# Attention on one core: all 96 query and key rows loaded into every sixth partition, by SyncE, with no row copies on chip

## The chip, the cores and the metric

The kernel runs on one core of a Trainium2 chip. The metric is the device time of one execution, in microseconds (us). Engines are named as the profile names them: PE (TensorE, PEld is its weight load), DVE (VectorE), ACT (ScalarE), POOL (GpSimd) and SP (SyncE, which here only issues DMAs). "ACTq" and "SPq" are the DMA-issuing instructions of ACT and SP.

## The reference, cut to what matters

The input is x [16 batches, 512 places, 256 channels]. A layer norm with a modulation per batch gives h; attention with 16 heads of width 16 follows, then a norm with a gate, then a mixture of 8 experts of which 2 are taken. The attention part, whose scores are what this change touches, is

```
q, k, v = heads(h @ Wq + bq), heads(h @ Wk + bk), heads(h @ Wv + bv)
scores = einsum('bhqd,bhkd->bhqk', q, k)
rel_q = einsum('bhld,lrd->bhlr', q, pos_emb)      # pos_emb[l, r] = dist_emb[l - r + 255], clipped
rel_k = einsum('bhrd,lrd->bhlr', k, pos_emb)
probs = softmax((scores + rel_q + rel_k) / 4)
ctx = einsum('bhqk,bhkd->bhqd', probs, v)
```

Everything is float32. To multiply float32 numbers at bfloat16 speed with small error, q and k are each split into three bfloat16 parts, and a score is a sum over six pairs of parts: 6 pairs x 16 channels = 96 rows of one matmul.

## The kernel before

The program is a row of stages: modulation, projections (which also store the parts of q and k to memory), distances (which stores rel_q + rel_k as a matrix of 512x512 for each of the 256 heads, "the matrix", in r_scratch), attention, and experts. The change touches only the attention stage, which works through 256 heads (16 batches of 16), one after another.

**A head.** For each of four query tiles t, PE multiplies the 96 rows of the tile's queries (t_qa) with the 96 rows of the keys (t_kb) into one of two PSUM buffers (t_ps): `score`, L1060. DVE adds the matrix (t_r), negates, and takes the row minimum (t_low): `add`, L1153, a custom operation and a read of its accumulator, with a small MEMSET (L1152) ahead. `score` of tile k waits until `add` of tile k-2 has emptied the buffer. POOL subtracts the minimum for tiles 0 and 1 (L952), ACT for tiles 2 and 3 (L1205). PE transposes the result one head later (`turn`, L1072, four transposes a tile), ACT takes the exponential (L1215), and PE multiplies with the values (`weigh`, L1083). Per group of four heads there are also the row sums (PE L1094), their reciprocal (DVE L1163), its widening (POOL L966), a transpose (PE L1101), the scaling (DVE L1168) and the store (SPq L1024). So a group of four heads is 16 scores, 16 turns, two blocks of `weigh` of 16 recorded matmuls each, and one each of the rest; 64 groups make the stage.

**The rows.** t_qa and t_kb have 96 partitions and hold two batches. Six blocks of 16 partitions hold the parts of q in the order 0, 1, 2, 0, 1, 0 and those of k in the order 0, 0, 0, 1, 1, 2. Memory holds each part once, 48 rows for q and 48 for k. ACT loads 64 of the 96 rows of each (T_Q_LOADED and T_K_LOADED: one run of 32 rows and two of 16; each row is 8 KB for half a batch, eight heads), 12 DMAs a batch, one after each of the first twelve heads of the batch before. The other 32 rows are copied on chip: those of q by DVE (`copy_q`, L1176, two heads' worth in a copy, one copy in every other head, after tile 1), those of k by POOL (`copy_k`, L986, four heads' worth in a copy, four copies a batch). PE waits for both kinds (q_copied, k_copied) before a new group of four heads.

**The matrix.** SP loads 1 MiB a head in four DMAs of 256 KB (`load_r`, L1008) into a ring of six heads; the load of head n waits until `add` of head n-6 is done. The values (L1014) and the stores (L1024) go through the same SP queue.

**The start of the stage.** ACT issues the 12 loads of batch 0 while SP issues the first heads' matrix; DVE copies three times and POOL twice before the first score, and POOL twice more after it.

Of the kernel before, what the change touches and what calls it, by code (L numbers as in the profile page):

```python
# [20 lines left out]
F32 = mybir.dt.float32  # L21
# [7 lines left out]
H = 16  # L29
D = E // H  # L30
M = 256
KC = E // P
TT = S // P
# [49 lines left out]


A_RUNS, B_RUNS = rows_of(A_PARTS), rows_of(B_PARTS)

T_PAIR = 2 * D
T_Q_LOADED, T_Q_COPY = ((0, 0, T_PAIR), (4 * D, 2 * D, D), (5 * D, 0, D)), T_PAIR
T_K_LOADED, T_K_COPY = ((0, 0, T_PAIR), (2 * D, 2 * D, D), (3 * D, 0, D)), 2 * T_PAIR


def modulation(nc, ins, mod_d, tab_d):
# [763 lines left out]
def attention(nc, rows_d, v_d, r_d, cT_d, nb=NB):  # L856
# [6 lines left out]
    with ctx:  # L863
# [9 lines left out]
        GH = 4  # L873
# [26 lines left out]

        ident_zero = sem("t_ident_zero")
        ident_done = sem("t_ident_done")
        batch_loaded = [sem(f"t_batch_loaded{i}") for i in range(2)]
        BATCH = 16 * (len(T_Q_LOADED) + len(T_K_LOADED))
        K_PLACES, Q_FIRST = (10, 12, 15, 18), 10
        q_copied = sem("t_q_copied")
        k_copied = sem("t_k_copied")
        v_loaded = [sem(f"t_v_loaded{i}") for i in range(2)]
        v_copied = sem("t_v_copied")
        r_loaded = [sem(f"t_r_loaded{i}") for i in range(RR)]  # L910
# [13 lines left out]
        scaled = sem("t_scaled")  # L924
        ctx_stored = [sem(f"t_ctx_stored{i}") for i in range(CS)]
        STORE = 16 * GH

        def rounds(engine, step_of, heads_after):

# [10 lines left out]
        with nc.Block() as block:  # L940
            @block.gpsimd
            def _(pool):
                nc.gpsimd.memset(vx[:], 1.0).then_inc(ident_zero, 1)
                nc.gpsimd.memset(ident[:], 0.0).then_inc(ident_zero, 1)
                pool.wait_ge(ident_zero, 2)
                nc.gpsimd.affine_select(out=ident[:], in_=ident[:], compare_op=ALU.not_equal, fill=1.0,
                                        base=0, pattern=[[-1, P]], channel_multiplier=1).then_inc(ident_done, 1)

                def subtract(n, j, t):

                    pool.wait_ge(added, TT * n + t + 1)
                    nc.gpsimd.tensor_scalar(neg[:, j % RING, t, :], neg[:, j % RING, t, :],  # L952
                                            low[:, j % RING, t:t + 1], None, ALU.subtract).then_inc(pool_sub, 1)

                def copy_v(step, k):
                    G = 2 * step + k

                    pool.wait_ge(v_loaded[k], 16 * (step + 1))
                    later(pool, weighed, TT * (G - 1))
                    nc.gpsimd.tensor_copy(vx[:, k, :, :, 0, :], vv[:, k]).then_inc(v_copied, 1)  # L960

                def widen(G):

                    pool.wait_ge(inverted, G + 1)
                    later(pool, spread, G)
                    nc.gpsimd.tensor_copy(wide[:], inv[:].rearrange("p t j -> p (t j)").unsqueeze(2)  # L966
                                          .to_broadcast([P, GT, CT])).then_inc(widened, 1)

                def head(step, j):
                    n = U * step + j  # L970
                    fixed = isinstance(n, int)
                    if not fixed or n < NH:
                        for t in range(2):
                            subtract(n, j, t)
                    if j % GH == 1 and (not fixed or 2 * GH <= n):
                        widen(2 * step + j // GH - 2)
                    if j % GH == 1 and (not fixed or n < NH):
                        copy_v(step, j // GH)

                def copy_k(b, i, subtracted):  # L980
                    heads = slice(b % 2 * H + GH * i, b % 2 * H + GH * (i + 1))

                    if i % 2 == 0:
                        pool.wait_ge(batch_loaded[i // 2], BATCH * (b + 1))
                    later(pool, pool_sub, subtracted)
                    nc.gpsimd.tensor_copy(  # L986
                        kb[T_K_COPY:T_K_COPY + T_PAIR, :, heads, :].rearrange("r c h w -> r c (h w)").bitcast(F32),
                        kb[0:T_PAIR, :, heads, :].rearrange("r c h w -> r c (h w)").bitcast(F32)).then_inc(k_copied, 1)
                    pool.wait_ge(k_copied, BG * b + i + 1)

                pool.wait_ge(ident_done, 1)
                for i in range(BG):
                    copy_k(0, i, 0)
                for n in range(NH + GH + 2):
                    head(n // U, n % U)
                    for i, place in enumerate(K_PLACES):
                        b = (n - place) // H + 1
                        if (n - place) % H == 0 and 1 <= b < nb:
                            copy_k(b, i, 2 * (n + 1))

            @block.sync
            def _(sp):
# [24 lines left out]
                def batch(g, pair, u):  # L1027
                    b = 2 * pair + u
                    for j in range(H):
                        load_r(g, H * b + j, j)  # L1030
                        k = j // GH
                        if j % GH == 0:
                            load_v(b, k)
                        if j % GH == 1 and BG * b + k >= 4:
                            store(b + (k - 4) // BG, (k - 4) % BG)

# [16 lines left out]
            def _(pe):  # L1053
# [68 lines left out]
                        if k % GT == 9 and (not fixed or 0 <= G < NGR):  # L1122
                            widen(G)

                pe.wait_ge(q_copied, 2)
                pe.wait_ge(k_copied, 1)
                score(0, 0, 0)

                def batch(b, last=False):
                    for s in range(H // U):  # L1130
                        for j in range(U):
                            if j % GH == GH - 1 and not (last and s == H // U - 1 and j == U - 1):
                                pe.wait_ge(q_copied, 2 * (BG * b + (U * s + j) // GH + 2))
                                pe.wait_ge(k_copied, BG * b + (U * s + j) // GH + 2)
                            head(H // U * b + s, j)

                batch(0)
# [7 lines left out]
            def _(dve):  # L1145
# [21 lines left out]
                    dve.wait_ge(spread, G + 1)  # L1167
                    nc.vector.tensor_tensor(cs[:, G % CS, :], cs[:, G % CS, :], p_i[:], ALU.mult).then_inc(scaled, 1)  # L1168

                def copy_q(b, m):  # L1170
                    at = b % 2 * H + 2 * m
                    heads = slice(at, at + 2)

                    if m % 4 == 0:
                        dve.wait_ge(batch_loaded[m // 4], BATCH * (b + 1))
                    nc.vector.tensor_copy(  # L1176
                        qa[T_Q_COPY:T_Q_COPY + T_PAIR, 0, heads, :].rearrange("r h w -> r (h w)").bitcast(F32),
                        qa[0:T_PAIR, 0, heads, :].rearrange("r h w -> r (h w)").bitcast(F32)).then_inc(q_copied, 1)

                def head(step, j):  # L1180
                    n = U * step + j
                    fixed = isinstance(n, int)
                    for t in range(TT):
                        k = TT * j + t
                        if not fixed or n < NH:
                            add(n, j, t, step)
                        b, m = (n - Q_FIRST) // H + 1, (n - Q_FIRST) % H // 2
                        if t == 1 and n % 2 == 0 and b < nb:
                            copy_q(b, m)
                        G = 2 * step + k // GT - 2  # L1190
                        if k % GT == 5 and (not fixed or 0 <= G < NGR):
                            invert(G)
                        if k % GT == 11 and (not fixed or 0 <= G < NGR):
                            scale(G)

                for m in range((H - Q_FIRST) // 2):
                    copy_q(0, m)
                rounds(dve, head, GH + 3)

            @block.scalar  # L1200
            def _(act):
# [31 lines left out]
                    if j % GH == GH - 1 and (not fixed or 7 <= n):  # L1233
                        empty(2 * step + j // GH - 1)

                pieces = [(qa, rows_d[0], run) for run in T_Q_LOADED] + [(kb, rows_d[1], run) for run in T_K_LOADED]

                def load(b, half, piece):
                    u = b % 2
                    tensor, src, (row, stored, rows) = pieces[piece]  # L1240
                    first = H // 2 * half
                    act.dma_start(
                        tensor[row:row + rows, 0, u * H + first:u * H + first + H // 2, :].rearrange("r h w -> r (h w)"),
                        src[b, stored:stored + rows, first:first + H // 2].rearrange("r h w -> r (h w)")
                    ).then_inc(batch_loaded[half], 16)

                def batch(b, last=False):
                    for s in range(H // U):
                        for j in range(U):
                            head(H // U * b + s, j)  # L1250
                            at = U * s + j
                            if at < 2 * len(pieces) and not last:
                                if at == 0:

                                    later(act, scored, TT * H * b)
                                load(b + 1, at // len(pieces), at % len(pieces))

                for half in range(2):
                    for piece in range(len(pieces)):
                        load(0, half, piece)  # L1260
                batch(0)
                for b in range(1, nb - 1):
                    batch(b)
                batch(nb - 1, last=True)
                for j in range(GH):
                    head(NH // U, j)

# [572 lines left out]
```

## Time and profile before

| | us |
|---|---|
| median of 3 runs (2884.1 to 2892.21) | 2888.73 |
| the profiled execution's own time | 2886.97 |
| its span | 2885.2 |

| busy over the span | PE | DVE | ACT | POOL |
|---|---|---|---|---|
| us | 2521.4 | 2055.5 | 1627.6 | 1883.5 |
| share | 87% | 71% | 56% | 65% |

The attention stage lies between 1185.8 us (its first DMA) and about 2250 us. The shares over the span are means over stages with different limits, so only rows from inside the stage speak on this change. In the rows "idle before" is the idle time of the engine ahead of an instruction, with what ended it; a matmul's end is modelled, its start is recorded. Rows of the timeline merge neighbours of one kind (x4).

### The profile page before, as it was taken

What the parts mean: (1) busy time and instruction counts of PE and PEld (TensorE: products, weight loads), DVE (VectorE), ACT (ScalarE), POOL (GpSimd) and SP (SyncE); (2) the same over time, 40 slices, a digit from 0 to 9 for tenths busy, and PEclk for the clock granted to TensorE, in tenths of its full rate; (3) what the DMA queues carried; (4) which work ended last, traced back from release to release, by engine and by line L of the source; (5) the groups of instructions that cost most, each with busy time, mean ns of one, the idle gap of its engine ahead of it and who ended that gap; (6) DMA issues with size and microseconds to landing.
All of it is one profiled execution on the core that took longest, in us unless ns stands there. A gap on an engine that the chain in (4) does not pass through costs nothing. (4 is left out here: it accounts for less than half of the span.)

```text
span 2885.2 us, 53492 instructions
## 1 busy us (share of the span) xinstructions
PE 2521.4 (87%) x19084; PEld 1753.8 (61%) x19084; DVE 2055.5 (71%) x5771; ACT 1627.6 (56%) x2069; POOL 1883.5 (65%) x1535
## 2 busy tenths in 40 slices
PE   3988688788878888599999999999999499999998
PEld 1655477677767777366666666666666355555553
DVE  4767277667767777577777777777777388888885
ACT  1645556566556666277878778788877222222222
POOL 2333356565765564488888888888888356666664
PEclk7999777778778778599999999999999799999999
DMA  3688799999999999999999999999998312222210
GB/s 117 226 296 269 259 401 386 378 400 385 398 393 387 376 404 388 316 328 317 302 313 308 312 310 306 304 306 301 314 301 266 132 68 77 77 77 77 77 48 24
DMA packets 301960, 773.59 MB, mean 268 GB/s; under 512 B 37608, under 2 KB 104496, under 8 KB 258048
## 3 DMA queue, kind: packets, MB, share of 16 engines
q1 hardware_dynamic: 277152, 660.82, 66.6%
q10 hardware_dynamic: 17888, 86.27, 9.2%
q0 software_dynamic: 6656, 23.07, 2.3%
q8 instruction: 154, 2.52, 0.4%
q14 instruction: 110, 0.90, 0.1%
HBM read 417.39 MB, written 352.63 MB: 267 GB/s over the span
## 5 line engine op out<-in xcount | busy, mean ns | idle before, releaser
L952 POOL TENSOR_SCALAR t_neg<-t_neg,t_low 128x512 f32<-128x512 f32 x512 | 793.6, 1563 | 121.5 <-DVE t_low L1153 117.2
L1153 DVE CUSTOM_DVE_ANT_1 t_neg<-t_ps,t_r 128x512 f32<-128x512 f32 x1024 | 667.6, 686 | 250.5 <-issue 245.5
L1215 ACT ACTIVATE t_eT<-t_pt 128x1024 f32<-128x1024 f32 x512 | 524.3, 1024 | 211.6 <-PE t_pt L1072 211.0
L1072 PE MATMUL t_pt<-t_ident,t_neg 128*128 128x128 f32 x4096 | 617.3, 273 | 4.7 <-POOL t_neg L952 4.2
L1072 PEld LDWEIGHTS t_pt<-t_ident,t_neg 128*128 128x128 f32 x4096 | 516.4, 142 | 82.9 <-POOL t_neg L952 5.9
L1537 PE MATMUL e_pX<-e_we,e_h2T 128*128 128x512 f32 x1024 | 455.8, 596 | 14.3 <-DVE e_even L1745 14.3
L1060 PE MATMUL t_ps<-t_kb,t_qa 96*128 96x512 bf16 x1024 | 399.1, 390 | 62.0 <-DVE t_low L1153 37.2
L831 DVE TENSOR_TENSOR d_r<-d_pq,d_r 128x1024 f32<-128x1024 f32 x256 | 299.6, 1219 | 139.0 <-ACT d_r L804 103.8
L1205 ACT ACTIVATE t_neg<-t_neg,t_low 128x512 f32<-128x512 f32 x512 | 369.2, 721 | 46.3 <-DVE t_low L1153 46.3
L831 DVE TENSOR_TENSOR ad_nat<-d_pq,ad_nat 128x1024 f32<-128x1024 f32 x256 | 298.6, 1218 | 121.0 <-ACT ad_nat L804 99.5
L706 POOL COPY ad_nat<-ad_nat 32x2048 f32<-32x2048 f32 (+1 forms) x156 | 294.3, 1886 | 104.6 <-DMA ad_nat<-q_by_place_scratch 98.3
L804 ACT ACTIVATE ad_nat<-d_pk 128x1024 f32<-128x1024 f32 x256 | 251.7, 1024 | 182.4 <-PE d_pk L755 78.5
L804 ACT ACTIVATE d_r<-d_pk 128x1024 f32<-128x1024 f32 x256 | 251.1, 1025 | 152.4 <-DMA r_scratch<-d_r 80.1
L1537 PEld LDWEIGHTS e_pX<-e_we,e_h2T 128*128 128x128 f32 x1024 | 188.6, 190 | 234.8 <-issue 203.7
L743 PE MATMUL d_pq<-ad_tab,ad_nat 96*128 96x128 bf16 x3072 | 292.8, 251 | 19.8 <-DVE ad_nat L831 5.7
L743 PEld LDWEIGHTS d_pq<-ad_tab,ad_nat 96*128 96x128 bf16 x3072 | 229.4, 114 | 58.6 <-issue 24.8
L755 PE MATMUL d_pk<-ad_tab,d_k 96*128 96x128 bf16 x2048 | 178.7, 238 | 83.3 <-ACT ad_nat L804 47.3
L1083 PE MATMUL t_pc<-t_eT,t_vx 128*32 128x512 f32 x2048 | 246.2, 598 | 0.3 <-ACT t_eT L1215 0.3
L706 POOL COPY d_q<-d_q 32x2048 f32<-32x2048 f32 (+1 forms) x52 | 98.1, 1887 | 221.2 <-DMA d_q<-q_by_place_scratch 219.5
L1060 PEld LDWEIGHTS t_ps<-t_kb,t_qa 96*128 96x128 bf16 x1024 | 115.5, 113 | 207.4 <-issue 129.8
L755 PE MATMUL d_pk<-ad_tab,ad_k 96*128 96x128 bf16 x2048 | 202.0, 256 | 25.2 <-ACT ad_nat L804 11.9
L755 PEld LDWEIGHTS d_pk<-ad_tab,d_k 96*128 96x128 bf16 x2048 | 136.1, 106 | 110.0 <-ACT ad_nat L804 61.2
(156 smaller groups left out, 3269.6 us busy)
## 6 DMA issues: line engine op xcount, KB each, us to landing
t_r<-r_scratch SPq DMA_DIRECT2D x1024, 256.0 KB, 6.5
r_scratch<-d_r SPq DMA_DIRECT2D x128, 1024.0 KB, 9.3
r_scratch<-ad_nat SPq DMA_DIRECT2D x128, 1024.0 KB, 7.0
ad_nat<-q_by_place_scratch ACTq DMA_DIRECT2D x78, 256.0 KB, 6.3
q_rows_scratch<-a_part SPq DMA_DIRECT2D x16, 768.0 KB, 4.7
k_rows_scratch<-a_part SPq DMA_DIRECT2D x16, 768.0 KB, 6.7
q_by_place_scratch<-ad_nat SPq DMA_DIRECT2D x6, 2048.0 KB, 16.8
k_by_place_scratch<-ad_nat SPq DMA_DIRECT2D x6, 2048.0 KB, 19.4
```

What stands on the lines that cost most here:

```text
L706: nc.gpsimd.tensor_copy(x[row:row + rows].rearrange("r l n -> r (l n)").bitcast(F32), x[source:source + rows].rearrange("r l n -> r (l n)" ...
L743: last = nc.tensor.matmul(pq[n % 2][:, a, :], q[c][:, l % QW, :], rhs, start=True, stop=True)
L755: last = nc.tensor.matmul(pk[n % 2][:, a, :], k[u][:, c % QW, :], tab[:, at:at + TB], start=True, stop=True)
L804: nc.scalar.activation(r[i % 2][:, :, n * KR:(n + 1) * KR], pk[n % 2][:].rearrange("p r l -> p l r"), ACT.Copy).then_inc(k_out, 1)
L831: nc.vector.tensor_tensor(part, pq[n % 2][:], part, ALU.add).then_inc(q_added, 1)
L952: nc.gpsimd.tensor_scalar(neg[:, j % RING, t, :], neg[:, j % RING, t, :], low[:, j % RING, t:t + 1], None, ALU.subtract).then_inc(pool_sub, 1)
L1060: nc.tensor.matmul(p_s[t % 2][:], lhs, kb[:, :, n % SLOTS, :], start=True, stop=True).then_inc(scored, 1)
L1072: last = nc.tensor.transpose(p_t[t // 2][:, t % 2, c, :], neg[:, j % RING, t, c * P:(c + 1) * P], ident[:])
L1153: nc.vector.tensor_tensor_reduce(out=neg[:, j % RING, t, :].rearrange("p (c r) -> p c r", r=TB), in0=p_s[t % 2][:].rearrange("p (c r) -> p ...
L1205: nc.scalar.activation(neg[:, j % RING, t, :], neg[:, j % RING, t, :], ACT.Identity, bias=low[:, j % RING, t:t + 1], scale=-1.0).then_inc( ...
L1215: nc.scalar.activation(to, p_t[half][:], ACT.Exp, scale=(1.0 if half else -1.0)).then_inc(exped, 1)
L1537: last = nc.tensor.matmul(pX[n][:], h2T[:, u, k, t * P:(t + 1) * P], we[:, k, n * 2 * E:(n + 1) * 2 * E], start=(k == 0), stop=(k == KC - 1))
```

## The change

All 96 rows of q and of k are loaded, and nothing is copied on chip. The rows are laid out otherwise: pair i of the six pairs of parts goes to the partitions i, i+6, i+12, ... (`tensor[pair:ROWS:NPAIR]`), so each DMA writes 16 partitions that stand six apart; the sum over 96 rows is the same. A batch takes 24 DMAs of 16 rows (128 KB each), 3 MiB instead of 2 MiB. For batches after the first, SP issues them, two after the matrix loads of each of twelve heads, in the queue that the matrix uses. ACT issues those of batch 0 only. PE waits for a half batch's twelve DMAs once in eight heads. `copy_q`, `copy_k` and their semaphores are gone.

```diff
-T_Q_LOADED, T_Q_COPY = ((0, 0, T_PAIR), (4 * D, 2 * D, D), (5 * D, 0, D)), T_PAIR
-T_K_LOADED, T_K_COPY = ((0, 0, T_PAIR), (2 * D, 2 * D, D), (3 * D, 0, D)), 2 * T_PAIR
...
-        batch_loaded = [sem(f"t_batch_loaded{i}") for i in range(2)]
-        BATCH = 16 * (len(T_Q_LOADED) + len(T_K_LOADED))
-        K_PLACES, Q_FIRST = (10, 12, 15, 18), 10
+        batch_loaded = [[sem(f"t_batch_loaded{u}_{half}") for half in range(2)] for u in range(2)]
+        NPAIR = len(A_PARTS)
+        HALF = 16 * 2 * NPAIR
+        AHEAD = 6
...
+        def load_rows(engine, b, half, pair, x):
+
+            tensor, parts = ((qa, A_PARTS), (kb, B_PARTS))[x]
+            first = H // 2 * half
+            at = b % 2 * H + first
+            engine.dma_start(tensor[pair:ROWS:NPAIR, 0, at:at + H // 2, :].rearrange("d h w -> d (h w)"),
+                             rows_d[x][b, parts[pair] * D:(parts[pair] + 1) * D, first:first + H // 2
+                                       ].rearrange("d h w -> d (h w)")).then_inc(batch_loaded[b % 2][half], 16)
...
-                    for i, place in enumerate(K_PLACES):
-                        b = (n - place) // H + 1
-                        if (n - place) % H == 0 and 1 <= b < nb:
-                            copy_k(b, i, 2 * (n + 1))
...
+                        done, step = divmod(H * b + j - AHEAD, H)
+                        if 0 <= done < nb - 1 and step < 2 * NPAIR:
+                            if step == 0:
+
+                                later(sp, scored, TT * H * done)
+                            for x in range(2):
+                                load_rows(sp, done + 1, step // NPAIR, step % NPAIR, x)
...
-                pe.wait_ge(q_copied, 2)
-                pe.wait_ge(k_copied, 1)
+                pe.wait_ge(batch_loaded[0][0], HALF)
...
-                            if j % GH == GH - 1 and not (last and s == H // U - 1 and j == U - 1):
-                                pe.wait_ge(q_copied, 2 * (BG * b + (U * s + j) // GH + 2))
-                                pe.wait_ge(k_copied, BG * b + (U * s + j) // GH + 2)
+                            if j == U - 1 and not (last and s == H // U - 1):
+
+                                pe.wait_ge(batch_loaded[(b + s) % 2][1 - s], HALF * ((b + s) // 2 + 1))
...
-                        if t == 1 and n % 2 == 0 and b < nb:
-                            copy_q(b, m)
...
                 for half in range(2):
-                    for piece in range(len(pieces)):
-                        load(0, half, piece)
+                    for pair in range(NPAIR):
+                        for x in range(2):
+                            load_rows(act, 0, half, pair, x)
```

DVE, inside the attention stage before, around the copy after tile 1 of an even head (L1153 is `add`, L1152 its small MEMSET):

```order
L1153 ISA t_neg,t_low<-t_ps,t_r 128x512
L1153 ISA t_low 128x1
L1176 COPY t_qa<-t_qa 32x512
L1152 MEMSET t_tiny 128x1
L1153 ISA t_neg,t_low<-t_ps,t_r 128x512
L1153 ISA t_low 128x1
```

DVE, the same place of the changed kernel (`add` is L1146 there):

```order
L1146 ISA t_neg,t_low<-t_ps,t_r 128x512
L1146 ISA t_low 128x1
L1145 MEMSET t_tiny 128x1
L1146 ISA t_neg,t_low<-t_ps,t_r 128x512
L1146 ISA t_low 128x1
```

The copy between two adds is gone, and the adds stand next to each other; nothing else moves on DVE.

SP before, two groups of heads inside the stage (t_r is the matrix, t_v the values, ctx_scratch the stored context):

```order
L1008 DMA t_r<-r_scratch 128x512 x4
L1024 DMA ctx_scratch<-t_cs 16x512 x4
L1008 DMA t_r<-r_scratch 128x512 x12
L1014 DMA t_v<-v_scratch 128x256
L1008 DMA t_r<-r_scratch 128x512 x4
L1024 DMA ctx_scratch<-t_cs 16x512 x4
```

SP of the changed kernel, two heads with row loads and the store behind them (L995 is the matrix's load, L928 a row load, L1011 the store):

```order
L995 DMA t_r<-r_scratch 128x512 x4
L1001 DMA t_v<-v_scratch 128x256
L928 DMA t_qa<-q_rows_scratch 16x4096
L928 DMA t_kb<-k_rows_scratch 16x4096
L995 DMA t_r<-r_scratch 128x512 x4
L928 DMA t_qa<-q_rows_scratch 16x4096
L928 DMA t_kb<-k_rows_scratch 16x4096
L1011 DMA ctx_scratch<-t_cs 16x512 x4
```

Behind each head's four matrix loads now stand two row loads, in twelve heads of sixteen; the loads that ACT issued between its activations are gone.

POOL before, one piece of the stage (L952 is the subtraction, L966 widens, L960 copies the values):

```order
L960 COPY t_vx<-t_v 128x16x16
L952 TENSOR_SCALAR t_neg<-t_neg,t_low 128x512 x2
L986 COPY t_kb<-t_kb 32x1024
L952 TENSOR_SCALAR t_neg<-t_neg,t_low 128x512 x4
L986 COPY t_kb<-t_kb 32x1024
L952 TENSOR_SCALAR t_neg<-t_neg,t_low 128x512 x2
```

POOL of the changed kernel:

```order
L970 COPY t_wide<-t_inv 128x512
L964 COPY t_vx<-t_v 128x16x16
L956 TENSOR_SCALAR t_neg<-t_neg,t_low 128x512 x8
L970 COPY t_wide<-t_inv 128x512
L964 COPY t_vx<-t_v 128x16x16
```

The eight subtractions of a group of four heads now follow one another with no key copy between them.

## Rows read from the trace of the kernel before

**Rows 1.** Busy time by stretch, granted clock, DMA share, GB/s (distances; attention).
```profile
700.00:1260.00 560.00, 448.68 (x5042) 382.19 (x5044) 395.06 (x481) 324.29 (x342) 341.68 (x194) 0.76 0.99 377
1300.00:2200.00 900.00, 870.22 (x6630) 594.28 (x6629) 667.68 (x2869) 719.28 (x938) 791.03 (x608) 1.00 1.03 308
```

**Rows 2.** Waits from 1300 to 2200 us: who waited, us, times, longest.
```profile
DVE t_neg L1153 <- issue: 214.5, 111, 1.9
...
PE t_ps L1060 <- DVE t_low L1153: 29.8, 110, 0.5
```

**Rows 3.** Copies (ns min/median/max) and the subtraction's group (busy, mean).
```profile
L1176 DVE COPY t_qa<-t_qa x128: 416/418/1252, 1199.5 to 2217.0; 32x512 f32<-32x512 f32 x128
...
L986 POOL COPY t_kb<-t_kb x64: 1029/1032/1210, 1199.6 to 2195.1; 32x1024 f32<-32x1024 f32 x64
...
L952 POOL TENSOR_SCALAR t_neg<-t_neg,t_low 128x512 f32<-128x512 f32 x512 | 793.6, 1563 | 121.5 <-DVE t_low L1153 117.2
```

**Rows 4.** Timeline of PE, one group of four heads: start, us, instruction.
```profile
1504.12 1.92 PE L1083 MATMUL t_pc<-t_eT,t_vx 128*32 128x512 f32 x16
...
1509.73 0.38 PE L1060 MATMUL t_ps<-t_kb,t_qa 96*128 96x512 bf16 x1
...
1510.86 0.41 PE L1060 MATMUL t_ps<-t_kb,t_qa 96*128 96x512 bf16 x1 [0.31 <-DVE t_low L1153]
...
1515.49 0.38 PE L1060 MATMUL t_ps<-t_kb,t_qa 96*128 96x512 bf16 x1
...
1516.15 0.38 PE L1060 MATMUL t_ps<-t_kb,t_qa 96*128 96x512 bf16 x1
...
1517.19 0.41 PE L1060 MATMUL t_ps<-t_kb,t_qa 96*128 96x512 bf16 x1 [0.22 <-DVE t_low L1153]
...
1519.19 0.60 PE L1072 MATMUL t_pt<-t_ident,t_neg 128*128 128x128 f32 x4
...
1520.38 0.64 PE L1083 MATMUL t_pc<-t_eT,t_vx 128*32 128x512 f32 x4
```

**Rows 5.** Timeline of DVE in the same group, around copies and scaling.
```profile
1507.81 0.42 DVE L1176 COPY t_qa<-t_qa 32x512 f32<-32x512 f32 x1
1508.27 0.69 DVE L1153 CUSTOM_DVE_ANT_1 t_neg<-t_ps,t_r 128x512 f32<-128x512 f32 x1
...
1509.50 0.69 DVE L1168 TENSOR_TENSOR t_cs<-t_cs,t_pi 128x512 f32<-128x512 f32 x1
...
1515.99 0.42 DVE L1176 COPY t_qa<-t_qa 32x512 f32<-32x512 f32 x1
1516.44 0.69 DVE L1153 CUSTOM_DVE_ANT_1 t_neg<-t_ps,t_r 128x512 f32<-128x512 f32 x1
```

**Rows 6.** Timeline of POOL in the same group.
```profile
1515.39 3.11 POOL L952 TENSOR_SCALAR t_neg<-t_neg,t_low 128x512 f32<-128x512 f32 x2 [0.70 <-DVE t_low L1153]
1518.56 1.03 POOL L986 COPY t_kb<-t_kb 32x1024 f32<-32x1024 f32 x1
```

**Rows 7.** DMA queues: SP's waits (1300:2200); t_r's issue ns min/median/max; its landing.
```profile
SPq L1008 <- DVE t_low L1153: 264.8, 190, 3.5
...
L1008 SPq DMA_DIRECT2D t_r<-r_scratch x1024: 319/432/3526, 1185.8 to 2223.2; - x171
...
DMA to landing us min/median/max: 2.5/6.5/19.5
```

**Rows 8.** Start of the stage: two stretches, then the timeline.
```profile
1190.00:1206.00 16.00, 3.44 (x6) 0.60 (x6) 5.81 (x16) 1.21 (x2) 2.33 (x2) 0.50 1.03 186
1206.00:1214.00 8.00, 3.79 (x17) 2.71 (x17) 2.66 (x12) 2.46 (x4) 7.44 (x6) 0.53 1.06 387
...
1201.14 1.02 PE L1060 MATMUL t_ps<-t_kb,t_qa 96*128 96x512 bf16 x2 [24.82 <-DVE t_qa L1176]
...
1208.38 0.06 DVE L1152 MEMSET t_tiny<- 128x1 f32 x1 [3.00 <-DMA t_r<-r_scratch]
...
1208.63 4.66 POOL L952 TENSOR_SCALAR t_neg<-t_neg,t_low 128x512 f32<-128x512 f32 x3
```

More of the change, by code:

```diff
@@ L85 @@
 A_RUNS, B_RUNS = rows_of(A_PARTS), rows_of(B_PARTS)
-T_PAIR = 2 * D
-T_Q_LOADED, T_Q_COPY = ((0, 0, T_PAIR), (4 * D, 2 * D, D), (5 * D, 0, D)), T_PAIR
-T_K_LOADED, T_K_COPY = ((0, 0, T_PAIR), (2 * D, 2 * D, D), (3 * D, 0, D)), 2 * T_PAIR
 def modulation(nc, ins, mod_d, tab_d):
@@ L902, in attention @@
         ident_done = sem("t_ident_done")
-        batch_loaded = [sem(f"t_batch_loaded{i}") for i in range(2)]
-        BATCH = 16 * (len(T_Q_LOADED) + len(T_K_LOADED))
-        K_PLACES, Q_FIRST = (10, 12, 15, 18), 10
-        q_copied = sem("t_q_copied")
-        k_copied = sem("t_k_copied")
+        batch_loaded = [[sem(f"t_batch_loaded{u}_{half}") for half in range(2)] for u in range(2)]
+        NPAIR = len(A_PARTS)
+        HALF = 16 * 2 * NPAIR
+        AHEAD = 6
         v_loaded = [sem(f"t_v_loaded{i}") for i in range(2)]
@@ L978, in head @@
                         copy_v(step, j // GH)
[L980 to L989, printed above, removed]
                 pool.wait_ge(ident_done, 1)
-                for i in range(BG):
-                    copy_k(0, i, 0)
                 for n in range(NH + GH + 2):
                     head(n // U, n % U)
-                    for i, place in enumerate(K_PLACES):
-                        b = (n - place) // H + 1
-                        if (n - place) % H == 0 and 1 <= b < nb:
-                            copy_k(b, i, 2 * (n + 1))
             @block.sync
@@ L1168, in scale @@
                     nc.vector.tensor_tensor(cs[:, G % CS, :], cs[:, G % CS, :], p_i[:], ALU.mult).then_inc(scaled, 1)
[L1170 to L1178, printed above, removed]
                 def head(step, j):
@@ L1186, in head @@
                             add(n, j, t, step)
-                        b, m = (n - Q_FIRST) // H + 1, (n - Q_FIRST) % H // 2
-                        if t == 1 and n % 2 == 0 and b < nb:
-                            copy_q(b, m)
                         G = 2 * step + k // GT - 2
@@ L1194, in head @@
                             scale(G)
-                for m in range((H - Q_FIRST) // 2):
-                    copy_q(0, m)
                 rounds(dve, head, GH + 3)
@@ L1234, in head, with batch @@
                         empty(2 * step + j // GH - 1)
[L1236 to L1247, printed above, removed]
+                def batch(b):
                     for s in range(H // U):
@@ L1250, in batch @@
                             head(H // U * b + s, j)
[L1251 to L1256, printed above, removed]
                 for half in range(2):
-                    for piece in range(len(pieces)):
-                        load(0, half, piece)
+                    for pair in range(NPAIR):
+                        for x in range(2):
+                            load_rows(act, 0, half, pair, x)
                 batch(0)
@@ L1263, in _ @@
                     batch(b)
-                batch(nb - 1, last=True)
+                batch(nb - 1)
                 for j in range(GH):
```

## Prediction

> **What bounds the kernel now.** I read the busy time by stretch first, because the page's shares mix stages. From 1300 to 2200 us, well inside attention, PE is busy 870.2 of 900 us at the full granted clock (1.00, that is 2.4 GHz); POOL has 791.0, ACT 719.3, DVE 667.7 [rows 1]. So PE bounds the stage, and only an edit that shortens PE's sequence, or its waits, can change the time. Next the waits in that stretch. The largest entry, 214.5 us of DVE before `add`, is DVE idling through PE's `weigh` blocks (1.9 us each) and costs nothing. PE's own wait worth naming is 29.8 us in 110 waits for the row minimum that DVE writes, all at `score` [rows 2]. That is the buffer rule: a score waits until `add` two tiles back is done.
>
> Then the timeline of one group of four heads, to see where the wait arises. The group lasts 1520.38 - 1504.12 = 16.26 us [rows 4]; 64 of them are 1041 us. With its turn a score takes 1516.15 - 1515.49 = 0.66 us. Two intervals are longer with no extra PE work in them: 1516.15 to 1517.19 is 1.04 (0.38 too long) and 1509.73 to 1510.86 is 1.13 (0.47 too long). The profile prints idle times of 0.22 and 0.31 there, since a matmul's end is modelled; the starts are recorded, so I count by starts. That makes 0.85 us of stall in a group. DVE's timeline names the causes: ahead of the first stands the query copy at 1515.99, ahead of the second the scaling at 1509.50 [rows 5].
>
> **The change part by part, in attention's steady part.**
>
> DVE's query copies go: 128, median 418 ns [rows 3], two in a group. They are not alike. The one at 1515.99 holds back the add that starts at 1516.44, so that could start about 0.45 us earlier, and the adds behind it with it. The score at 1517.19 waits for that add. Without the copy it starts 0.66 after the last, at 1516.81: gain 0.38. The other copy, at 1507.81, comes where PE has other work (a transpose block). The add behind it, at 1508.27, is 0.46 late, but DVE then waits for a score anyway, and by the scaling at 1509.50 I see a few hundredths of that delay left. So the second stall of 0.47 stays almost whole, as scaling makes it; I credit 0.05. Together 0.43 us a group, 64 groups: 27.5 us. From below: the printed idle time alone, 0.22 x 64 = 14 us. From above: both stalls gone, 0.85 x 64 = 54 us.
>
> POOL's key copies go: 64 of 1.03 us [rows 3]. PE has no wait for POOL in the steady part (its named wait is for DVE) [rows 2], so this is worth nothing there. What hides them is that a head's subtractions are wanted one head later. It matters as cover: when PE loses its 0.38, the turn of the head's second tile, now at 1519.19 [rows 4], comes at about 1518.8, and POOL's two subtractions from 1515.39 end at 1518.50 [rows 6]. About 0.3 us remains. Without key copies POOL needs 8 x 1.56 + 1.0 = 13.5 us of a group that becomes 15.8, so it keeps up.
>
> The loads move from ACT's queue to SP's and grow from 12 to 24 a batch. SP's issue: 0.43 us each [rows 7], so 0.86 us more in each of twelve heads of sixteen, mean 2.6 us a group. SP waits for `add` 264.8 us of 900, 4.8 us a group [rows 7], so it fits. Behind a row load stand the next head's matrix loads, which DVE waits for. A matrix load is issued when the ring frees it, five to six heads ahead of its use (5 x 4.07 = 20 us), and lands after a median 6.5 us [rows 7]. Two row loads ahead of it in the same ring of the same engines cost 0.26 MB; at 387 GB/s [rows 8] that is 0.7 us, at 186 GB/s 1.4 us. Twelve heads of 1.4 us, if nothing is recovered between, are 17 us, more than the 13.5 that the 20 leave behind the landing; at 0.7 us it is 8 us, which fits. The total asked for: 308 GB/s now [rows 1], plus 65 KB a head (1 MiB in 16 heads) and a shorter period, (16.26 - 0.43) / 4 = 3.96 us a head: (308 GB/s x 4.07 us + 65.5 KB) / 3.96 us = 333 GB/s; in the heads with row loads, which carry 262 KB of rows and not the mean of 197, it is 350. The distances stage moved 377 over 560 us [rows 1]. So I put this at nothing, with two rivals for it. PE's waits for rows are then for loads issued some ten heads (40 us) ahead: nothing. Nothing of ACT's is late: it waits for PE.
>
> **The start of the stage.** Here two bounds stand far apart. Before, the first score starts at 1201.14 after copies; DVE then waits 3.0 us for the second head's matrix at 1208.38, and POOL, busy with key copies until the second half landed, first subtracts at 1208.63 [rows 8]. While rows land, the DMA engines move only 186 GB/s, at a share of 1.03; once only the matrix lands, 387. By 1208.4 about 4.65 MB have moved (20 us at 186, 2.4 at 387). Now 1.05 MB more stand in front. If the new loads are as slow as the old, that is 5.6 us later: a loss of 5.6. If they run at 387, 5.7 MB take 14.7 us, to 1200.7: a gain of 7.7. In either case the copies are gone from the path, POOL's worth most (its first subtraction starts 7.5 us after the first score, though one add of 0.69 us is all that it needs). I take a gain of 4, somewhat on the side of 387, since the copies' part is certain.
>
> The Trainium skill has a rule for the 186 (page "SBUF — State Buffer", section on the DMA port swizzle): what a transfer reaches is set by its partitions, 16 neighbours reach 4 of 16 ports and 32 reach 8, with 104 and 189 GB/s measured. By its formula 16 partitions six apart reach 13 or 14 ports. The trace agrees as far as it goes: 186 while such blocks land, 387 after. By that rule the start gains 7.7 and the time would be 2852.
>
> **Sum.** 2886.97 (the profiled execution) - 27.5 - 4 = 2855.5; that execution lies 1.8 us, 0.06%, under the median of the runs shown, which I leave out. Forecast 2856, 1.1% faster. Its own range from the bounds: 2887 - 54 - 8 = 2825 to 2887 - 14 + 6 = 2879; the middle of it, 2842 to 2868, is where I expect it if the mechanism holds.
>
> **Rivals.**
>
> *The transfers become the bound (slower).* Place: the matrix load of heads whose queue carries rows; DVE's `add` waits for it and PE for DVE. It decides if the engines can't move over 333 GB/s here. For it: the DMA share is 1.03 at 308 already, and the matrix comes in 2 KB rows. Against: 387 at the start of this very stage, and SP waits for the ring 29% of the time, so the ring and not the transfers set its pace. Price if 308 is the ceiling: 277 MB in 900 us become 291.5, 946 us; 46 x 1041/900 = 54 us slower: 2941. The skill's page "DMA: Bandwidth & Descriptors" (Specifications) gives about 358 GB/s as a core's share of memory. Rows 1 and 8, with 377 and 387, contradict it as a ceiling here; by it the loading heads, at 350, would be just carried.
>
> *Rows make the matrix late in the last heads of each load block.* The 1.4 us a head above: 17 against 13.5 us of slack, 3.5 lost in each of 15 batches would be 50, of which most is recovered in the four heads without rows; I price it at 20: 2876.
>
> *DVE has slack and the stall returns elsewhere (no change).* PE, 0.38 earlier, meets POOL's subtraction, whose margin is 0.3, or the scaling's stall grows by what the first loses. Then only the start is left: 2883.
>
> *Both stalls go.* If the scaling's stall is fed by the copy's delay more than I read, 0.85 a group: 2887 - 54 - 4 = 2829.
>
> **Numbers.** Chances: forecast 0.70, transfers bound 0.07, late matrix 0.08, no change 0.07, both stalls 0.08. Range for 8 in 10: 2834 to 2880; it leaves out the first rival, part of "no change" and part of the last. A measurement of this kernel can tell 0.3%, 8.7 us, from no change. Faster by more: 0.70 + 0.08 + 0.08 = 0.86; within: 0.07; slower: 0.07.
>
> **What would show it.** Right: a group of four heads lasts 15.8 us; one wait of PE for the row minimum in a group instead of two, at the scaling; the copies' groups absent; t_r still landing well ahead, with no DVE wait for it after the start; the first head's adds at about 1197 to 1200; GB/s of 325 to 335 in the stage. Wrong: DVE waits that end with a landing of t_r in the middle of batches (first and second rival); PE turns that wait for POOL (third); a start at 1206 or later (the 186 GB/s were not the narrow loads'). The forecast fails as a whole if the stage's period stays at 16.26.

## The result: 3.3% slower

The changed kernel takes 2985.13 us (median of 4 runs, 2979.45 to 2987.92) against 2888.48 us; the ratio is 1.0333, 95% interval 1.0312 to 1.0354. The forecast was 2856, faster. The span of its profiled execution is 2983.2 us. It is 98 us longer than before, of which 93 lie between the first and the last `add` of the attention stage (1136.4 us, before 1043.0) and 4 ahead of the stage, in code that the change does not touch.

### The profile page after: what moved, and what is told of

The parts are those of the page before. It is cut to its first block and busy times, and to the rows that moved or that the text cites. A ratio compares the mean times of both kernels' runs of the same rounds, so it can differ in the third digit from the quotient of the medians.

```text
span 2983.2 us, 53368 instructions
## 1 busy us (share of the span) xinstructions
PE 2545.9 (85%) x19084; PEld 1756.0 (59%) x19084; DVE 2001.8 (67%) x5643; ACT 1634.5 (55%) x2069; POOL 1817.8 (61%) x1471
## 5 line engine op out<-in xcount | busy, mean ns | idle before, releaser
L1146 DVE CUSTOM_DVE_ANT_1 t_neg<-t_ps,t_r 128x512 f32<-128x512 f32 x1024 | 670.4, 686 | 234.4 <-issue 234.2
L1077 PE MATMUL t_pc<-t_eT,t_vx 128*32 128x512 f32 x2048 | 255.9, 619 | 0.3 <-ACT t_eT L1193 0.3
```

What stands on the lines that cost most here:

```text
L1146: nc.vector.tensor_tensor_reduce(out=neg[:, j % RING, t, :].rearrange("p (c r) -> p c r", r=TB), in0=p_s[t % 2][:].rearrange("p (c r) -> p ...
```

## The profile after

The same stretch as in [rows 1], 1300 to 2200 us; columns as there:

```profile
1300.00:2200.00 900.00, 807.11 (x6051) 540.86 (x6050) 568.24 (x2517) 663.64 (x859) 670.92 (x506) 0.99 1.03 295
```

PE is busy 63 us less, at nearly the same clock (0.99, before 1.00), since it has fewer heads to work on in the stretch. The DMA share is 1.03 as before, yet the DMA engines move 295 GB/s, not 308. That is the first thing to see: more is asked for and less is moved.

The waits of the same stretch, who waited for whom, us, times, longest:

```profile
DVE t_tiny L1145 <- PE t_ps L1054: 99.5, 50, 3.0
...
PE t_ps L1054 <- DVE t_low L1146: 90.7, 94, 2.9
...
DVE t_tiny L1145 <- issue: 70.7, 38, 3.6
```

and SP's own:

```profile
SPq L995 <- DVE t_low L1146: 32.7, 82, 1.4
```

PE's wait for the row minimum is three times that of [rows 2]. DVE has 170 us of new waits ahead of the small MEMSET, which is the instruction that stands behind the wait for the matrix (t_r). The profile names PE or nothing as the releaser, but PE's score had ended; the landing events of the matrix's semaphores show the cause. Call margin the time from the landing of a head's last matrix load to the head's first `add`. Before, it was 9 to 14 us on average, by the head's place in its batch. Now it is 0.1 to 0.7 us on average in heads 9 to 15 of a batch and in heads 0 and 1 of the next (the first batch, and the last, which has no row loads beside it, left out). In 110 of the 256 heads `add` starts within 0.2 us of the landing, before in 3. SP, which waited 264.8 us for the ring [rows 7], waits 32.7: the transfers, not the ring, set its pace.

SP's timeline in a bad stretch, with the waits of PE and DVE beside it:

```profile
1676.42 2.61 SPq L928 DMA_DIRECT2D t_qa<-q_rows_scratch  x1
...
1679.08 0.59 SPq L928 DMA_DIRECT2D t_kb<-k_rows_scratch  x1
...
1679.71 1.97 SPq L1011 DMA_DIRECT2D ctx_scratch<-t_cs  x4
...
1681.72 2.77 SPq L995 DMA_DIRECT2D t_r<-r_scratch  x4
...
1681.97 0.41 PE L1054 MATMUL t_ps<-t_kb,t_qa 96*128 96x512 bf16 x1 [2.01 <-DVE t_low L1146]
...
1684.53 0.50 SPq L928 DMA_DIRECT2D t_qa<-q_rows_scratch  x1
1685.07 0.59 SPq L928 DMA_DIRECT2D t_kb<-k_rows_scratch  x1
...
1685.70 2.00 SPq L995 DMA_DIRECT2D t_r<-r_scratch  x4
1685.83 0.06 DVE L1145 MEMSET t_tiny<- 128x1 f32 x1 [2.06 <-PE t_ps L1054]
```

SP issues without a pause. A row load's issue is mostly 0.5 to 0.6 us, but the one at 1676.42 takes 2.61. That fits a queue that takes no more for the moment; the profile does not name the cause.

A group of heads that nothing disturbs, PE's timeline of the changed kernel:

```profile
1643.15 0.41 PE L1054 MATMUL t_ps<-t_kb,t_qa 96*128 96x512 bf16 x1
...
1646.24 0.38 PE L1054 MATMUL t_ps<-t_kb,t_qa 96*128 96x512 bf16 x1
1646.90 0.38 PE L1054 MATMUL t_ps<-t_kb,t_qa 96*128 96x512 bf16 x1
1647.98 0.41 PE L1054 MATMUL t_ps<-t_kb,t_qa 96*128 96x512 bf16 x1 [0.26 <-DVE t_low L1146]
...
1649.42 1.92 PE L1077 MATMUL t_pc<-t_eT,t_vx 128*32 128x512 f32 x16
...
1665.54 1.92 PE L1077 MATMUL t_pc<-t_eT,t_vx 128*32 128x512 f32 x16
```

The stall that the scaling causes is there as forecast (1.08 between the last two starts, before 1.13 [rows 4]). The other one is gone. But the shortest groups last 16.12 us (from one `weigh` block at 1649.42 to the same one of the next group at 1665.54), not the forecast 15.83. Experiment e9 shows where the 0.29 us went.

The start, POOL, PE and DVE:

```profile
1204.64 1.02 PE L1054 MATMUL t_ps<-t_kb,t_qa 96*128 96x512 bf16 x2 [24.52 <-DMA t_kb<-k_rows_scratch]
...
1206.16 6.25 POOL L956 TENSOR_SCALAR t_neg<-t_neg,t_low 128x512 f32<-128x512 f32 x4 [14.76 <-DVE t_low L1146]
...
1208.49 0.06 DVE L1145 MEMSET t_tiny<- 128x1 f32 x1 [0.48 <-DMA t_r<-r_scratch]
```

The stage begins 4.1 us later than before, at 1189.88. Counted from there the second head's `add` comes at 18.6 us, before at 22.6: the 4 us taken for the start. But this is one execution. The kernels of e1, e4, e7, e9 and e11 below begin the stage with the same code, and in their profiled executions the same `add` comes at 20.6 to 22.0 us, 0.6 to 2.0 less than before. While the rows land, the DMA engines move 271 GB/s, at a share of 0.97, where the kernel before had 186 [rows 8]:

```profile
1190.00:1204.00 14.00, 0.00 (x0) 0.00 (x0) 0.00 (x0) 0.00 (x0) 1.26 (x3) 0.50 0.97 271
```

## Experiments

Each stands against its own runs of the kernel before (medians 2888.5 to 2892.6). "Six apart" is the changed kernel's form, a load of 16 rows into every sixth partition; "MiB" are those of rows a batch. e3, e4, e7, e8 and e9 leave out part of the work.

| run | rows: form, queue, MiB a batch | us | ratio (95%) |
|---|---|---|---|
| changed kernel | six apart, SP, 3 | 2985.1 | 1.0333 (1.0312 to 1.0354) |
| e1 | six apart, ACT, 3 | 2888.0 | 0.9998 (0.9986 to 1.0011) |
| e2 | blocks of 16, SP, 3 | 3152.3 | 1.0929 (1.0891 to 1.0967) |
| e3 | old loads, ACT, 2, no copies | 2901.7 | 1.0033 (1.0020 to 1.0047) |
| e4 | six apart, half width, SP, 1.5 | 2882.9 | 0.9977 (0.9964 to 0.9990) |
| e5 | long runs, SP, 3 | 3058.5 | 1.0579 (1.0553 to 1.0605) |
| e6 | long runs, ACT, 3 | 3011.5 | 1.0419 (1.0401 to 1.0436) |
| e7 | six apart, SP, 2 | 2889.2 | 0.9990 (0.9977 to 1.0003) |
| e8 | old loads, SP, 2, no copies | 2934.2 | 1.0152 (1.0132 to 1.0172) |
| v1 | two apart, ACT, 2.5, keys copied | 2878.6 | 0.9955 (0.9938 to 0.9972) |
| e9 | e4 with a short ACT copy | 2870.7 | 0.9933 (0.9912 to 0.9954) |
| e10 | changed, 1/4 of matrix by ACT | 2982.4 | 1.0319 (1.0302 to 1.0336) |
| e11 | changed, rows between matrix loads | 2929.8 | 1.0123 (1.0091 to 1.0155) |

**e1: the queue.** 

```diff
-                            for x in range(2):
-                                load_rows(sp, done + 1, step // NPAIR, step % NPAIR, x)
...
+                            if b + 1 < nb:
...
+                                load_step(act, b + 1, U * s + j)
```

> The changed kernel with its row loads (24 a batch, 16 rows six partitions apart, 3 MiB) issued by ACT in ACT's own queue for all batches, two behind each of the first twelve heads. Theory Q (the matrix's queue: SP never waits for the ring any more, 32.7 us of 900 where it was 264.8, so its row by row issue and the rows standing ahead of the matrix are the price): the matrix lands in time again, about 2860 us. Theory B (bytes: the transfers were within a few per cent of their ceiling before, and 1 MiB more a batch costs its time in any queue): 16.8 MB at about 300 GB/s, 56 us or more over the kernel before, 2940 to 2985. Theory S (the rows six partitions apart are what is dear, in any queue): about 2985.

2888.0: all 97 us come back with the same bytes in the same form. Theory Q holds in this, though it expected 2860. Its stretch from 1300 to 2200:

```profile
1300.00:2200.00 900.00, 872.62 (x6630) 591.36 (x6626) 625.92 (x2764) 726.08 (x939) 733.63 (x553) 1.00 1.04 324
```

324 GB/s at a share of 1.04. Theory B in its simple form falls (the DMA engines can carry 3 MiB a batch), and S falls. What remains is that the same packets go through faster from a queue of their own. But it is no gain either: the mean margin of the matrix is down to 2.5 to 8 us, `add` still starts within 0.2 us of the landing in 25 heads, and the last group of a batch lasts 16.74 us on average.

**e2: blocks of 16.**

```diff
-            engine.dma_start(tensor[pair:ROWS:NPAIR, 0, at:at + H // 2, :].rearrange("d h w -> d (h w)"),
...
+            return [(x, pair * D, 1, D, (A_PARTS, B_PARTS)[x][pair] * D) for pair in range(NPAIR) for x in range(2)]
```

> The changed kernel with the six parts in six blocks of 16 neighbouring partitions again; number of DMAs (24 a batch), bytes, queue and order as in the changed kernel. Theory S: issue falls from 0.5 to 0.6 us to 0.43 us or less and the time to under 2900 us. Theories Q and B: within 1% of 2985 us; if the spread over partitions helps the transfers, as the prediction took it, even slower, 3000 or more.

3152.3, with 266 GB/s in the stretch:

```profile
1300.00:2200.00 900.00, 757.88 (x5416) 496.07 (x5416) 511.30 (x2264) 594.64 (x768) 601.24 (x452) 0.95 1.05 266
```

Theory S had the sign wrong: the spread over partitions saves 167 us in SP's queue, of which 19 lie ahead of the second head's `add` (37.4 us after the first load here, 18.6 in the changed kernel). The spread does cost issue time (ACT's loads at the start: 0.61 us each, 0.44 in this run), which e4 shows to cost nothing in SP.

**e3: what the copies cost alone.**

```diff
+            if b < 2:
+                return [(x, row, 1, rows, stored) for x in range(2) for row, stored, rows in (A_RUNS, B_RUNS)[x]]
+            return [(x, row, 1, rows, stored) for x in range(2) for row, stored, rows in (T_Q_LOADED, T_K_LOADED)[x]]
```

> The kernel before's loads (64 of 96 rows, 2 MiB a batch, ACT's queue, one DMA a head) and no copies on chip: the first two batches load all 96 rows, later ones leave the other 32 rows as they are, so this leaves out part of the rows' refresh. It measures what the copies cost alone. The prediction's steady term says 27.5 us less than before, 2861 us; with the start's gain 2857. If the stall goes elsewhere: 2880 to 2889.

2901.7, slower than with the copies; neither expectation held. The undisturbed group is 16.12 us here too. So e3 does not price the copies alone. The start, which loads 96 rows in blocks, is 5.9 us later at the second head (28.5 us after the first load, before 22.6), about the prediction's bound for slow loads (5.6). The first batch, beside which batch 1's 96 rows are loaded in the same form, lasts 74.7 us, before 68.0. Nine of the other fourteen batches last 64.5 us (before 65.2), and five up to 3.7 us more. In those the matrix is late. Over all batches after the first its mean margin is 2 to 7 us where the same loads left 9 to 14, and SP's wait for the ring, 264.8 us before, is 86.2:

```profile
SPq L1017 <- DVE t_low L1161: 86.2, 120, 2.8
```

The rate is 308 GB/s as before. With rows in this form the transfers had little left, and a group 1% shorter used it up: the kernel before stood near the edge of the transfers without a wait showing it.

**e4: half the bytes, all the DMAs.**

```diff
-            wide = H // 2
+            wide = H // 2 if b < 2 else H // 4
```

> The changed kernel with each row load half as wide (4 heads instead of 8, 4 KB a row) after the second batch: as many DMAs in the same queue and order, but 1.5 MiB a batch; it leaves out half of the rows. Theory B: bytes are under those of before, so 2860 to 2870 us. Theory Q as a matter of issue time (24 issues of 0.5 to 0.6 us in SP): 2940 to 2985. Theory S as a matter of issue: the same 2940 or more; as a matter of transfer: 2900 to 2930.

2882.9: the 24 issues a batch in SP cost nothing; bytes or packet size do. The share falls to 0.94, the margin is 11 to 14 us on average in all heads. Theory B's 2860 to 2870 is missed for two reasons: the group is 16.12 us (e9), and the first batch, beside which the rows of the next are loaded whole, lasts 72.8 us and the second 66.5, the others 64.5.

**e7: two thirds of the bytes, 8 KB packets.**

```diff
+            npair = NPAIR if b < 2 else 4
```

> The changed kernel with four of the six pairs loaded after the second batch (16 DMAs and 2 MiB a batch, rows of 8 KB six apart, SP); it leaves out a third of the rows. Theory QB (the ring shared with the matrix carries only so much, so the price comes from bytes in it once they pass a limit between 1.5 and 3 MiB a batch): between the half-width run's 2883 and 2985, nearer the first, 2880 to 2900. Theory W (the 8 KB packets ahead of the matrix are the price, whatever the sum of bytes): two thirds of the loss, about 2950.

2889.2, so the packet size is not it (theory W falls). In SP's queue 2 MiB a batch fit, at 312 GB/s; 3 MiB don't. From the third batch on every batch lasts 64.5 us; the first, beside which six pairs are loaded, and the second take 71.3 and 72.0, which uses up what the others gain on the 65.2 of before.

**e5, e6, e8: form and queue crossed.** The lines shown are of e5 and e6; e8 has the loads of e3.

```diff
-            engine.dma_start(tensor[pair:ROWS:NPAIR, 0, at:at + H // 2, :].rearrange("d h w -> d (h w)"),
...
+            return [(x, row, 1, rows, stored) for x in range(2) for row, stored, rows in (A_RUNS, B_RUNS)[x]]
```

> The changed kernel with the rows in blocks, loaded in the longest runs (48, 32, 16 rows; 14 DMAs and 3 MiB a batch) by SP. If the number of issues or of narrow DMAs is what made the 16-row blocks cost 3152 us, this is well under it: about 3000 to 3050. If only the spread over partitions counts (a DMA of 32 or 48 neighbouring rows is spread twice as far as one of 16): about 3050. If blocks are slow in any size: 3150.

> The same 14 loads in blocks, 3 MiB a batch, in ACT's queue. Theory S' (rows in blocks cost transfer time in either queue, the spread of six saves it): slower than the strided loads in ACT's queue (2888), about 2930. If the queue alone decides: 2888 again.

> The kernel before's loads (2 MiB a batch in blocks of 32 and 16 rows, 12 DMAs) issued by SP, no copies; it leaves out the refresh of the other 32 rows. The blocks cost ring time in the shared queue: over the 2902 us that the same loads take in ACT's queue, 2930 to 2960. If the queue matters only above 2 MiB: 2900.

3058.5, 3011.5 and 2934.2; e6 is 80 us above the 2930 expected of theory S'. At 3 MiB the long runs cost 123 us over six apart in ACT's queue and 73 in SP's (blocks of 16: 167), of which 6 and 9 lie at the start. Being in SP's queue costs 97 us six apart and 47 in runs, and 33 with the old loads. e6 says it in one row; the DMA engines are as full as ever and carry 287 GB/s:

```profile
1300.00:2200.00 900.00, 799.22 (x5880) 536.21 (x5872) 553.42 (x2449) 644.62 (x835) 651.96 (x491) 0.97 1.04 287
```

PE's granted clock in the stretch is 0.97 here and in e5, and 0.95 in e2. What part of these prices the lower clock has is not separated.

**e10: relief for the ring.**

```diff
+                            if H * b + U * s + j + RR < NH:
+                                load_r(act, H * b + U * s + j + RR, NT - 1)
```

> The changed kernel, rows as they are (strided, 3 MiB a batch, SP), but one of the four matrix loads of each head issued by ACT in its queue, so bytes and DMAs are the same and 256 KB a head leave SP's ring. Theory R (one ring carries only some 296 GB/s where two together carry 324): the matrix lands in time again, 2885 to 2895 us. If what counts is that row packets stand ahead of matrix packets in one ring: three quarters of the loss stay, 2950 or more.

2982.4: almost nothing came back. The second head's `add` comes 7 us later than in the changed kernel (26.0 us after the first load), since ACT's matrix loads stand behind the first rows; so up to 10 of the 97 us may have come back behind the start. The queues of its stretch, SP's first, then ACT's (packets, MB, share of 16 engines):

```profile
q1 hardware_dynamic: 111477, 213.58, 82.5%
q10 hardware_dynamic: 29267, 53.27, 20.6%
```

Two queues share the work and still make 298 GB/s. ACT is not what is late: in 232 of the 256 heads its part is issued before SP's last one. So it is not one queue's capacity; what counts at 3 MiB is that the row loads stand in the matrix's queue.

**e11: the order inside the queue.**

```diff
                     for c in range(NT):
+                        if more and c in (1, 3):
+                            load_rows(sp, done + 1, step // NPAIR, step % NPAIR, c // 2)
```

> The changed kernel with each head's two row loads not behind its four matrix loads but between them (one ahead of the second, one ahead of the fourth); queue, bytes, DMAs and issue times as in the changed kernel. Theory C (two row DMAs back to back, to the same 16 partitions, let the engines fall out of step, and the ring behind waits for the slowest): at least a third of the 97 us comes back, under 2950 us. If the mere presence of row packets in the matrix's ring costs: 2975 to 2990.

2929.8, 55 of the 97 us back from moving each row load by a few places, at 311 GB/s in the stretch:

```profile
1300.00:2200.00 900.00, 840.82 (x6347) 567.24 (x6349) 599.27 (x2649) 692.50 (x900) 703.41 (x528) 1.00 1.04 311
```

Two row loads back to back, behind a head's matrix loads, are dearer than two between them, by over half of the queue's price. The edit parts the two and also moves them ahead of other transfers; which of the two counts is not separated. That the engines fall out of step behind the pair is my reading of it, not shown.

**e9: where the rest of the copies' gain went.** PE and ACT of e4 in a group that no transfer disturbs:

```profile
1504.90 1.01 ACT L1208 ACTIVATE t_eT<-t_pt 128x1024 f32<-128x1024 f32 x1
...
1505.81 0.59 ACT L1214 ACTIVATE t_cs<-t_pc 128x512 f32<-128x512 f32 x1
...
1506.28 0.73 ACT L1198 ACTIVATE t_neg<-t_neg,t_low 128x512 f32<-128x512 f32 x1
...
1506.89 1.03 ACT L1208 ACTIVATE t_eT<-t_pt 128x1024 f32<-128x1024 f32 x1
...
1507.62 0.38 PE L1069 MATMUL t_ps<-t_kb,t_qa 96*128 96x512 bf16 x1
...
1508.07 0.63 PE L1081 MATMUL t_pt<-t_ident,t_neg 128*128 128x128 f32 x4
...
1510.49 0.41 PE L1069 MATMUL t_ps<-t_kb,t_qa 96*128 96x512 bf16 x1
```

The same two scores of the kernel before, around the `weigh` block of [rows 4]:

```profile
1503.37 0.38 PE L1060 MATMUL t_ps<-t_kb,t_qa 96*128 96x512 bf16 x1
...
1505.98 0.41 PE L1060 MATMUL t_ps<-t_kb,t_qa 96*128 96x512 bf16 x1
```

ACT works through exponential, context copy (t_cs), subtraction and exponential without a gap. A turn mostly starts 0.22 us after its score; here it starts 0.45 after, when the exponential at 1506.89 has ended and freed the half of PSUM that the turn writes. The interval from that score over the next `weigh` block is 2.87 us, before 2.61.

```diff
-                    nc.scalar.activation(cs[:, G % CS, :], p_c[:], ACT.Copy).then_inc(emptied, 1)
+                    some = S if G < CS else S // 4
+                    nc.scalar.activation(cs[:, G % CS, 0:some], p_c[:, 0:some], ACT.Copy).then_inc(emptied, 1)
```

> The half-width kernel, in which no transfer is late, with ACT's copy of the context out of PSUM cut to a quarter of its columns after the third group (0.6 us becomes 0.3 or less); it leaves out that part of the context. Theory A (with DVE's copy gone PE runs into ACT, whose subtraction, exponentials and this copy follow each other without a gap there, and 0.25 + 0.04 us of the 0.43 are lost again): the group of 16.12 us falls to about 15.85, 15 to 18 us less than the half-width kernel's 2883. If POOL's four subtractions in a row are what PE meets: unchanged at 16.12.

The `weigh` blocks at one place of a group, in e9:

```profile
1502.67 1.92 PE L1092 MATMUL t_pc<-t_eT,t_vx 128*32 128x512 f32 x16
...
1518.53 1.92 PE L1092 MATMUL t_pc<-t_eT,t_vx 128*32 128x512 f32 x16
```

The group is 15.86 us, the forecast 15.83, and the time 12 us under e4 (15 to 18 expected; the two profiled executions are 15.5 apart). So PE ran into ACT's context copy: 0.26 of the missing 0.29 us go with it.

**v1: a version that beats both.** Queries loaded whole, so that DVE copies nothing; keys copied by POOL as before; parts in every second partition; ACT's queue.

```diff
+T_Q_LOADED = (0, 0), (1, D), (T_PAIR, 0), (T_PAIR + 1, D), (2 * T_PAIR, 2 * D), (2 * T_PAIR + 1, 0)
+T_K_LOADED, T_K_COPY = ((0, 0), (1, D), (T_PAIR, 2 * D), (T_PAIR + 1, 0)), 2 * T_PAIR
...
+                        tensor[row:row + T_PAIR - row % 2:2, 0, u * H + first:u * H + first + H // 2, :]
```

> A middle way: all query rows loaded (no DVE copies), the key rows copied by POOL as before; parts in every second partition; 20 DMAs and 2.5 MiB a batch, ACT's queue. PE's group of four heads should last 16.12 us as in the kernels without copies, and the matrix should land in time: 64 x 0.14 = 9 us less than before, 2880 us. If the transfers are late already: 2890.

2878.6, 0.9955 (0.9938 to 0.9972): about 13 us faster than before, a little more than the 9 of PE's groups (11 when whole batches are compared, 65.2 us before and 64.5 here).

```profile
1300.00:2200.00 900.00, 881.77 (x6705) 598.11 (x6698) 632.92 (x2790) 731.79 (x950) 801.12 (x615) 1.00 1.02 319
```

319 GB/s with the matrix 7.5 to 15 us ahead, more than the kernel before had at 308 with rows in blocks.

## Why the prediction was wrong

*The loads move and grow: "I put this at nothing".* This is the step that failed, by about 100 us. It set 333 GB/s against the 377 and 387 of [rows 1, 8]. Both are rates of other mixes: the distances stage, and eight microseconds of the start with the matrix alone. In this stage no run moved more than 324 over 900 us, and what is moved depends on the rows: 266 (blocks of 16, SP), 287 (runs, ACT), 295 (six apart, SP), 311 (the same, not back to back), 324 (six apart, ACT), each at a share of 1.03 to 1.05. The share of 1.03 in [rows 1] was for the rival and was set aside. Both slower rivals saw what happened: the transfers bind, and the matrix is late in the heads whose loads stand behind rows. The first one's price, 54 us, took 308 as ceiling; with the measured 295 its own sum gives 291.5 MB in 988 us, 102 us slower, near the measured 93 in the stage. SP's waits for the ring, read as 29% of free capacity, were no reserve: in e3, with the same loads and a group 1% shorter, 86.2 of the 264.8 us were left.

*The gain from the copies: 0.43 us a group.* Right in its mechanism: the stall of 0.38 is gone in every kernel without the query copy, and that of the scaling is 0.05 smaller (1.08). Mis-sized in its sum: PE then meets ACT's context copy, and 0.14 us remain, 9 us (11 by whole batches) and not 27.5. The prediction asked what is late next, looked at POOL's margin of 0.3 us, and dismissed ACT with "it waits for PE". ACT does wait for PE elsewhere in the group; in this place it has no gap. The third rival, a stall that returns elsewhere, named the wrong engine.

*POOL's key copies: nothing.* Right: v1 keeps them, and its group is 16.12 us as without them.

*Start: 4 us gained.* It came out in the one profile of this kernel (18.6 against 22.6 us), but five kernels with the same start gained 0.6 to 2.0, so the size was partly luck. The rows landed at 271 GB/s, neither the 186 nor the 387 of the two bounds. The first head's adds, forecast for 1197 to 1200, came at 1205.3, or 1201.2 without the stage's later beginning. The gain is gone by head 16, whose first `add` comes 3.3 us later than before, counted from the first load, since the matrix is late by then. With the rows in blocks (e3) it is a loss of 5.9, close to the other bound. The Trainium skill's rule of how far a transfer's partitions are spread (page "SBUF — State Buffer", the DMA port swizzle) agrees with the runs in its order: in SP's queue 16 neighbours are slowest (3152 us), long runs next (3058), six apart fastest (2985), and in ACT's queue, where blocks of 16 were not tried, long runs (3011) are slower than six apart (2888). Queue and place of such a transfer count nearly as much here (e1, e11).

*Still open.* Why row loads in the matrix's queue slow all transfers at 3 MiB a batch, and at 2 MiB only with rows in blocks (e8), not six apart (e7). e10 excludes the queue's capacity, e4 the number of issues, e7 the packet size alone; e11 shows that their place inside the queue is part of it. The 40 us that e11 leaves are not explained, nor is the spread of the start between executions.

## What to carry to other kernels

Take a DMA share of about 1 as a full resource, even when no engine waits for a transfer. It does not tell the ceiling in GB/s (266 to 324 here): take that from the same stage and mix, and expect added bytes to cost. The place of a transfer can matter as much as its size: in this kernel small loads with few rows did best in a queue of their own, or between the large ones, with their rows spread over the partitions. When a stall of the bounding engine goes, look at the very instants behind it on every engine: an engine with 20% idle time can still be the next bound in one place of the loop.

## What the runs showed of the hardware

- The same 3 MiB of rows a batch: 266 to 324 GB/s in the stage, by form, queue and order, at a DMA share of 1.03 to 1.05.
- A DMA whose 16 rows stand six partitions apart took 0.49 to 0.61 us to issue, one of 16 or 32 neighbouring rows 0.31 on ACT while the stage ran (0.44 at its start).
- Two such DMAs back to back behind a head's matrix loads, or each between two of them: 2985 against 2930 us.
